# A decoder layer with routed experts: gates found at the routed steps, last rows turned by TensorE, returned rows loaded in pairs and combined by VectorE alone

## The reference

```python
x = _layernorm(x + _L0_xattn_ref(x, ctx_1024, L0_xattn_learnable_matrix), axis=-1)
x = _layernorm(x + _L0_ffn_ref(x, ...), axis=-1)

def _L0_ffn_ref(x, shared_w1, shared_w2, experts_w1, experts_w2, gate_w):
    shared = jnp.einsum('td,dh->th', x_flat, shared_w1.T)
    shared = jnp.einsum('th,hd->td', jax.nn.silu(shared), shared_w2.T)
    gate_logits = x_flat @ gate_w.T
    top_k_gates, top_k_idx = jax.lax.top_k(gate_logits, TOP_K)
    top_k_gates = jax.nn.softmax(top_k_gates, axis=1)
    gates = gates.at[jnp.arange(T)[:, None], top_k_idx].set(top_k_gates)
    h = jnp.einsum('td,ehd->teh', x_flat, experts_w1)
    expert_out = jnp.einsum('teh,edh->ted', jax.nn.silu(h), experts_w2)
    selected = jnp.einsum('ted,te->td', expert_out, gates)
    return (shared + selected).reshape(B, S, D)
```

## Time and profile before

| | us |
|---|---|
| median of 3 runs | 852.23 |
| lowest, highest | 851.64, 852.59 |
| the profiled execution | 854.55 |
| its span in the trace | 852.4 |
| TensorE matmul busy | 793.0 (93%) |
| VectorE busy | 549.4 (64%) |
| ScalarE busy | 525.1 (62%) |
| GpSimd busy | 313.4 (37%) |

### The profile page before, as it was taken

The page is one execution under the profiler, slowest core; times in us unless marked ns, Lnnn a source line. Parts: engine busy times, 40 slices in busy tenths (PEclk is TensorE's granted clock), DMA queues, the critical chain, the costliest instruction groups (busy, mean ns, idle before and its releaser), DMA issues. The chain is left out here.

```text
span 852.4 us, 19205 instructions
## 1 busy us (share of the span) xinstructions
PE 793.0 (93%) x7234; PEld 480.1 (56%) x7235; DVE 549.4 (64%) x1019; ACT 525.1 (62%) x788; POOL 313.4 (37%) x233
## 2 busy tenths in 40 slices
PE   5899999999999999999999796899999999999992
PEld 2367333333333333333332585788888888877871
DVE  4575789999999999999970495873333333212365
ACT  4441687777887787777889486454444444423475
POOL 5040594555433335555550112042333333310153
PEclk9999899999999999999999998999999999999997
DMA  9683244234344443334132697743432222212342
GB/s 298 123 217 141 111 150 137 94 102 137 132 149 150 149 149 116 100 116 172 59 113 112 250 368 179 303 82 63 76 80 74 74 74 74 70 52 66 97 148 98
DMA packets 72647, 111.95 MB, mean 131 GB/s; under 512 B 41725, under 2 KB 56254, under 8 KB 68222
## 3 DMA queue, kind: packets, MB, share of 16 engines
q1 hardware_dynamic: 67422, 93.88, 36.3%
q0 software_dynamic: 4816, 16.65, 5.7%
q10 hardware_dynamic: 336, 0.40, 0.4%
HBM read 66.60 MB, written 32.37 MB: 116 GB/s over the span
## 5 line engine op out<-in xcount | busy, mean ns | idle before, releaser
L169 DVE TENSOR_REDUCE partial<-ring 128x1 f32<-128x512 f32 (+3 forms) x509 | 308.8, 668 | 30.8 <-PE ring L151 21.6
L692 ACT ACTIVATE probs<-scores 128x1024 f32<-128x1024 f32 (+1 forms) x320 | 271.2, 905 | 63.4 <-PE scores L739 32.6
L755 PE MATMUL acc<-probs,values 128*32 128x512 f32 (+3 forms) x1280 | 170.1, 541 | 0.9 <-ACT acc_sb L697 0.7
L1666 DVE TENSOR_TENSOR work<-hid,work 128x512 f16<-128x512 f32 (+1 forms) x112 | 76.1, 682 | 136.3 <-ACT work L1269 112.9
L1264 ACT ACTIVATE hid<-turned 128x512 f32<-128x512 f32 (+1 forms) x112 | 65.3, 583 | 148.9 <-PE turned L1423 117.4
L1448 PE MATMUL ops<-weights,work 128*128 (+1 forms) x1320 | 149.5, 273 | 5.6 <-DVE work L1666 3.0
L151 PE MATMUL ring<-kstack,qstack 48*128 48x512 f16 (+1 forms) x580 | 144.8, 352 | 2.2
L1423 PE MATMUL turned<-mats,weights 128*128 128x256 f16 (+1 forms) x1344 | 144.6, 262 | 2.3 <-DMA mats<-attn 1.2
L1448 PEld LDWEIGHTS ops<-weights,work 128*128 128x128 f16 x1320 | 127.9, 98 | 22.9 <-issue 3.8
L667 POOL TENSOR_TENSOR a_w_in<-a_w_in,w_scale 128x2304 f32<-128x2304 f32 x16 | 64.4, 4027 | 207.2 <-DMA a_w_in<-w_all 207.2
L1423 PEld LDWEIGHTS turned<-mats,weights 128*128 (+1 forms) x1344 | 122.6, 98 | 21.3 <-issue 4.0
(11 more groups left out here) (201 smaller groups left out, 714.4 us busy)
## 6 DMA issues: line engine op xcount, KB each, us to landing
a_w_in<-w_all SPq DMA_DIRECT2D x16, 1152.0 KB, 7.9
w_split_d<-a_w_out SPq DMA_DIRECT2D x16, 1152.0 KB, 5.6
weights<-w_split_d SPq DMA_DIRECT2D x6, 2048.0 KB, 20.2
weights<-w_split_d POOLq DMA_DIRECT2D x3, 2048.0 KB, 11.1
qstack<-q_split SPq DMA_DIRECT2D x72, 64.0 KB, 2.6
kstack<-k_split SPq DMA_DIRECT2D x72, 64.0 KB, 2.7
weights<-by_token SPq DMA_DIRECT2D x16, 256.0 KB, 5.5
attn<-xT SPq DMA_DIRECT2D x4, 512.0 KB, 7.6
```

Source lines behind the costliest of these rows:

```text
L169: return nc.vector.tensor_reduce(out=found[:, places[0]:places[-1] + 1:step], in_=bank[:, 0:WIDTH[n]].rearrange("p (k w) -> p k w", k=len( ...
L692: nc.scalar.activation(probs[:, s % 2, at:at + w], scores[half][:, first:first + w], ACT.Exp, scale=QK_SCALE).then_inc(exp_done, 1)
L755: mm = nc.tensor.matmul(acc[VW * j:VW * (j + 1), QB - w:QB], values[:, h, k0 + j], probs[:, s % 2, at:at + w], start=first, stop=last)
L1666: nc.vector.tensor_tensor(hid[:, parity, 1, chunks, 0:w], hid32[:, b % 2].rearrange("p (j n) -> p j n", n=TW)[:, :, 0:w], hid[:, parity, 0 ...
```

## The change

1. The last item of the second layer norm no longer feeds the gates by DMA. TensorE turns its f32 rows (`turn_last`), VectorE splits them into `lastT`, and `multiply_gates` reads them there. ScalarE's first halves of these rows come behind step 1's hidden halves, the second halves move from VectorE to GpSimd, and SyncE has two transposing DMAs fewer; its store of the last quarter of `rows_d` waits for those second halves.
2. The exponential is taken at step `H0` on ScalarE, the gates are found at step `H0 + 1` on VectorE.
3. The one-hot columns are made by 16 tensor_scalar operations with a scalar per partition instead of one or two over all tiles. A few other small operations of VectorE change their form (`nmean`, `f_veps`, `f_nmean`).
4. A token's two results lie side by side in `by_token`, and one load brings both for a chunk: 8 loads of 512 KB. Four of them stand ahead of the turn for step 27.
5. VectorE multiplies by the gates and adds in one operation for each tile and choice. `scale` on ScalarE and the adding on GpSimd are gone.
6. Chunks are combined in steps 24, 25 and 26 (2, 3 and 3), and the final scaling of chunks 0 to 4 stands in steps 25 and 26.

```diff
+        lastT = region(QB, DC * QB).bitcast(f16).rearrange("p (a c n) -> p a c n", a=2, c=DC)
-        part16 = sb("part16", [P, 2, 2, NT], f16)
+        part32 = sb("part32", [P, 2, 2, NT], f32)
-        returned = weights[:, 0, 0:NC * 2 * TB * D * 2].bitcast(f32).rearrange("p (c r t d) -> p c r t d", c=NC, r=2, t=TB)
+        returned = weights[:, 0, 0:NC * 2 * TB * D * 2].bitcast(f32).rearrange("p (c t r d) -> p c t r d", c=NC, r=2, t=TB)
+        last_ps = ops[1][:].rearrange("p t d -> p (t d)").rearrange("p (c n) -> p c n", c=DC)
-        SCALED_IN = {F0: (0, 1), F0 + 1: (2, 3, 4, 5), F0 + 2: (6, 7)}
-        COMBINED_IN = {F0 + 1: (0, 1, 2, 3), F0 + 2: (4, 5, 6, 7)}
+        COMBINED_IN = {F0: (0, 1), F0 + 1: (2, 3, 4), F0 + 2: (5, 6, 7)}
+        FINAL_IN = {F0 + 1: (0, 1), F0 + 2: (2, 3, 4)}
...
@@ SyncE
-            for n in range(NC):
-                if n < LAST_HALVES:
-                    sp.wait_ge(x16_lo, n + 1)
-                else:
-                    sp.wait_ge(x16_lo_last, n - LAST_HALVES + 1)
+            for n in range(LAST_HALVES):
+                sp.wait_ge(x16_lo, n + 1)
...
             for g in range(NQ):
+                sp.wait_ge(x16_lo, (g + 1) * TPQ // TB)
...
+            def take_back(c):
+                sp.dma_start(returned[:, c], by_token[c * TW * 2:(c + 1) * TW * 2, :].rearrange("(t p r) d -> p t r d", p=P, r=2)
+                             ).then_inc(returned_in[c], 16)
+
-            for n in range(R0, NALL):
+            for n in range(R0, NALL - 1):
                 step(n, n % 2)
-
             for i in range(2):
                 sp.wait_ge(rows_out[i], 16 * sum(groups(n) for n in range(R0, F0) if n % 2 == i))
-            for c in range(NC):
-                for r in range(2):
-                    sp.dma_start(returned[:, c, r],
-                                 by_token[r * S + c * TW:r * S + (c + 1) * TW, :].rearrange("(t p) d -> p t d", p=P)
-                                 ).then_inc(returned_in[c], 16)
+            for c in range(NC // 2):
+                take_back(c)
+            step(NALL - 1, (NALL - 1) % 2)
+            for c in range(NC // 2, NC):
+                take_back(c)
@@ GpSimd
-            pool.wait_ge(allT_in[NC - 1], 16)
+            pool.wait_ge(allT_in[LAST_HALVES - 1], 16)
             for e in range(LOADED_FIRST, NE - 2):
                 load_expert(nc.gpsimd, e, late_in)
+            for n in range(LAST_HALVES, NC):
+                pool.wait_ge(x16_hi, n + 1)
+                second_halves_of_rows(nc.gpsimd, n).then_inc(x16_lo, 1)
...
-            for c in range(NC):
-                pool.wait_ge(scaled, 2 * TB * (c + 1))
-                nc.gpsimd.tensor_tensor(returned[:, c, 0], returned[:, c, 0], returned[:, c, 1], ALU.add).then_inc(pair_added, 1)
-                if c >= 2:
-                    find_scale(c - 2, (c - 2) * TB, (c - 1) * TB)
-            find_scale(NC - 2, (NC - 2) * TB, (NC - 1) * TB)
+            for c in range(NC - 1):
+                find_scale(c, c * TB, (c + 1) * TB)
@@ ScalarE
-                if n >= NQ:
+                if NQ <= n < NM - 1:
                     first_halves(n - NQ)
...
-                if isinstance(n, int) and n in SCALED_IN:
-                    for c in SCALED_IN[n]:
-                        scale(c)
-                if isinstance(n, int) and n == F0 + 2:
-                    for c in range(FINAL_AHEAD):
+                if isinstance(n, int) and n == 0:
+                    first_halves(NQ - 1)
+                if isinstance(n, int) and n == H0:
+                    act.wait_ge(gap_found, 1)
+                    nc.scalar.activation(gap_exp[:], gap[:], ACT.Exp).then_inc(gap_exp_done, 1)
+                if isinstance(n, int) and n in FINAL_IN:
+                    for c in FINAL_IN[n]:
                         final(c)
@@ TensorE
+            def turn_last():
+
+                pe.wait_ge(added, NM)
+                pe.wait_ge(ln_done, NM)
+                for c in range(DC):
+                    for t in range(TPQ):
+                        mm = nc.tensor.transpose(last_ps[:, c, t * P:(t + 1) * P], res[:, NT - TPQ + t, c * P:(c + 1) * P], ident32[:])
+                mm.then_inc(last_turned, 1)
+
...
             widen(0, 0)
+            turn_last()
             in_turn(pe, step, 0, NALL)
@@ VectorE
-                nc.vector.tensor_tensor(nmean[:, n % 2], nought[:].broadcast_to([P, TPQ]), mean_var[:, n % 2, :, 0],
-                                        ALU.subtract).then_inc(nmean_done, 1)
+                nc.vector.tensor_scalar(nmean[:, n % 2], mean_var[:, n % 2, :, 0], -1.0, None, ALU.mult).then_inc(nmean_done, 1)
...
+                for t in range(NT):
+                    one_hot = nc.vector.tensor_scalar(in_column[:, r, t], columns16[:, 0], part32[:, 0, r, t:t + 1], None, ALU.is_equal)
+                then(one_hot)
...
             def combine(c):
-                dve.wait_ge(pair_added, c + 1)
+
+                dve.wait_ge(returned_in[c], 16)
+                dve.wait_ge(gates_step, 3)
...
-                nc.vector.tensor_tensor(res[:, tiles], res[:, tiles], returned[:, c, 0], ALU.add).then_inc(combined, 1)
+                for r in range(2):
+                    for t in range(TB):
+                        tile = c * TB + t
+                        if r == 1:
+                            dve.wait_ge(combined, c * 2 * TB + t + 1)
+                        nc.vector.scalar_tensor_tensor(out=res[:, tile], in0=returned[:, c, t, r], scalar=gates[:, r, tile:tile + 1],
+                                                       in1=res[:, tile], op0=ALU.mult, op1=ALU.add).then_inc(combined, 1)
...
+                if isinstance(n, int) and n == H0 + 1:
+                    find_gates()
+
+            dve.wait_ge(last_turned, 1)
+            nc.vector.tensor_copy(lastT[:, 0], last_ps).then_inc(last_hi, 1)
+            dve.wait_ge(last_hi, 1)
+            nc.vector.tensor_tensor(lastT[:, 1], last_ps, lastT[:, 0], ALU.subtract).then_inc(last_lo, 1)
...
-            find_gates()
             in_turn(dve, step, 0, NALL)
```

More of the change, by code:

```diff
@@ L1275, in final @@
                                          scale=f_rstd[:, t:t + 1]).then_inc(act_final, 1)
-            def scale(c):
-                act.wait_ge(returned_in[c], 32)
-                for r in range(2):
-                    for t in range(TB):
-                        tile = c * TB + t
-                        nc.scalar.activation(returned[:, c, r, t], returned[:, c, r, t], ACT.Copy,
-                                             scale=gates[:, r, tile:tile + 1]).then_inc(scaled, 1)
             def step(n, parity):
@@ L1708, in find_moments @@
                 dve.wait_ge(f_aggr_done, last_tile)
[L1709 to L1712 removed]
+                nc.vector.tensor_scalar(f_veps[:, tiles], f_mean_var[:, tiles, 1], EPS, None, ALU.add).then_inc(f_var_done, 1)
+                nc.vector.tensor_scalar(f_nmean[:, tiles], f_mean_var[:, tiles, 0], -1.0, None, ALU.mult).then_inc(f_nmean_done, 1)
             def step(n, parity):
```

67 lines of the change are left out of this document (24 added, 43 removed).

## The result

The changed kernel took 844.16 us (median of 4 runs, 843.48 to 845.32), the kernel before, run beside it, 852.41: a ratio of 0.990, 95% interval 0.989 to 0.992. Forecast were 846.3. Run once more later, beside other kernels, it took 846.38 (6 runs, 843.66 to 848.99; ratio 0.993, 0.991 to 0.995). The ten runs together have a median of 844.9. The difference between the two medians is itself a finding of this study (experiments 9 and 10).

What follows compares the result with a forecast made beforehand. The prediction took TensorE alone to bound 566 to 818 us, with small routing work in the head and VectorE in the tail. Head -3.0 and tail -2.9 took 5.9 off the median 852.23: 846.3, range 843 to 848.5.

Steps and rivals of the forecast that it cites:

- both halves: The head (routing up to step 4) gains 3.0 us and the tail (combining returned rows) 2.9; chance 0.55.
- (1): Head: ScalarE's last two first halves, 1.15 us, move later; step 0's SiLU starts at 521.35 instead of 522.5.
- (3): Head: ScalarE no longer stands at the exponential, so placing starts at 536.4 instead of 540.01, -3.6 us.
- (4): Head: finding the gates leaves VectorE, 0.6 us, making -4.2; two later table loads cost nothing.
- (2): Head: TensorE's eight transposes fit its idling; choosing starts at 529.25 instead of 531.01, -1.75 us.
- (5): Head: GpSimd's last two second halves run beside placing and stall VectorE, +1.2 us.
- (6): Head: each one-hot, as 16 small operations, takes 1.5 us, -0.8 each; range -0.8 to +1.2 each.
- (7): Head: nmean and f_veps as one-input tensor_scalar count 0, with -2.2 us kept for the range.
- (8): Tail: the last send lands at 801.2, the first load pair takes 6.4 us, the first chunk starts at 807.6.
- (9): Tail: ScalarE's scaling and GpSimd's adding vanish; VectorE pays +6.8 us in all, 3.0 a chunk (2.7 to 3.3).
- (10): Tail: with chunks spread over steps 24 to 26, take 26 starts at 837.3 instead of 840.14; tail -2.9 us.
- Rival E: Slower: VectorE, alone with the returned rows, becomes the tail's bound; 854.3 us with no head gain; chance 0.07.

Runs made afterwards that it cites:

- experiment 9: Changed kernel with one-hots as before and last halves moved earlier: 843.1 us; beside it the changed kernel (846.38) and before (851.63) were run and profiled again.
- experiment 10: Experiment 9's combined version plus eight idle TensorE matmuls behind narrowing 2: 841.89 us, ratio 0.988.
- experiment 5: Changed kernel with the exponential between step 0's and step 1's SiLU and the gates found before spreading, as before: 847.07 us, ratio 0.994.
- experiment 6: Changed kernel with the last rows turned by DMA and their second halves on VectorE, as before: 844.51 us, ratio 0.990.
- experiment 4: Changed kernel with all eight loads of returned rows behind the turn for step 27: 849.41 us, ratio 0.996.
- experiment 3: Changed kernel with VectorE combining in steps 25 and 26 only, final scaling of chunks 0 to 3 in step 26: 849.9 us, ratio 0.998.
- experiment 7: Changed kernel with one-hot columns by one or two broadcast operations, as before: 844.19 us, ratio 0.991.
- experiment 2: Changed kernel with the tail of before (ScalarE scales, GpSimd adds, separate loads), so the head's change alone: 849.54 us, ratio 0.997.
- experiment 8: Changed kernel with the last rows' first halves between step 0's banks and GpSimd's second halves beside choosing: 843.69 us, ratio 0.990.

## Why the prediction was right, and where it was not

The forecast, 846.3 with both halves paying, was the case that came true; 844.16 lies in its own range of 843 to 848.5, and the second median, 846.38, on the forecast itself. That the sum is this close is in part luck: in the first profile the head gave 1.9 for 3.0 and the tail 6.5 for 2.9, two misses that go against each other. In the second pair of profiles it was 0.7 and 4.0, with 1.7 of slower clock in step 4.

(1), (3), (4) held: ScalarE without the exponential, hidden halves in time, placing 3.1 earlier for 3.6, 0.6 less on VectorE without the gates, two table loads without effect. Experiment 5 prices (3) and (4) at 2.4 when taken back.

(2) was -1.3 for -1.75: the eight transposes took 1.94 us where I had 1.5, VectorE's cast stands behind them, and between the logits' copy and choosing there are 0.75 us where I had half a one. Experiment 6 has 2.3 for the whole part before its stall, of which 1.1 is a slower clock in that execution.

(5) was 1.7 where I took 1.2, the single stall "and a little". It was two stalls, 0.83 at the cast and 0.89 at the hidden halves, together less than the 2.3 that I had for two. The range held it.

**(6) failed.** I took 0.09 us apart from two operations of 128x32 in 0.27. It was 0.16 (2.69 for 16): the 128x128 copy's 0.13, which I had set aside, was the nearer row, and it was still too low. The reason given for the smaller row, a quarter of the bytes, was wrong too: 128 f16 numbers are 256 bytes, twice those of 32 f32 and half those of 128 f32. The Trainium skill ("VectorE: DVE Perf Modes", the TRN2 errata) advised against such small tiles, with an estimate of 0.19 each and 3.0 for 16 by its constants; the trace agrees that the small tiles cost more, 2.69 against 2.28, and lies below the estimate. My sum had -1.6 for it, and it was +0.7. Of the 3.3 us by which the token numbers missed the forecast, 2.3 are this.

(7) held. `nmean` as tensor_scalar still waits for GpSimd, VectorE and GpSimd of the changed kernel:

```profile
509.13 2.27 POOL L1064 TENSOR_TENSOR weights<-res,weights 128x512 f16<-128x512 f32 x2 [2.87 <-ACT weights L1245]
509.17 1.15 DVE L1496 TENSOR_SCALAR nmean<-mean_var 128x4 f32<-128x4 f32 x1
```

1.15 us for four numbers, as 1.07 in the earlier trace rows. The Trainium skill ("SBUF — State Buffer", "Who interferes with whom") lists tensor_scalar and cast among what can take both ports; the cast of 1.03 in (5) is the same case, and the trace agrees for both. The delays I added for the gather (+1) and the clock (+0.6) were not in the first profile: from token numbers to step 4 it took 8.7 us, and 9.3 before (9.7 in its second profile). Delays of this kind come and go: 9.7 us and a widening of 7.08 in the changed kernel's second profile, 10.2 in experiment 4. The last loads of experts 7 and 6 moved 426 to 433 GB/s from 550 to 555 us in both profiles of the changed kernel and in experiment 4, but 429 and 424 also in experiments 3 and 7, where from token numbers to step 4 it took 8.6; whether they are what delays the gather was not settled.

**(8) was the term that made the difference.** From step 4's start I had the first chunk at 241.2 us; it was at 237.7, 3.4 earlier. 1.0 of it is the send, which had landed within 1.5 us of its issue where I took 2.2, near the middle of a bound 5 us wide; 2.4 are the load, 512 KB within 4.0 us, where I kept 6.4 from a pair of loads with fourteen behind it. I had named larger pieces as a reason for less and left it in the range alone. But the 6.4 was also a slow one of its kind. The same first pair, scaled by ScalarE, in the second profile of before (asked for at 801.77) and in experiment 2 (asked for at 800.38):

```profile
807.40 3.30 ACT L1282 ACTIVATE weights<-weights,gates 128x256 f32<-128x256 f32 x8 [5.75 <-DMA weights<-by_token]
```

```profile
805.17 3.51 ACT L1284 ACTIVATE weights<-weights,gates 128x256 f32<-128x256 f32 x8 [4.90 <-DMA weights<-by_token]
```

That is 5.6 and 4.8 us, and in experiment 4 one load of 512 KB with seven behind it took 5.1. So the size of the pieces is not shown to be what made the load quick; a single row had priced the term. What I missed altogether was that with the loads in their old place VectorE itself would have stood before the first chunk (experiment 4).

(9) held: 2.85 a chunk in a range of 2.7 to 3.3, with 0.40 between operations where I had 0.34, and `f_veps` at 0.17 without a stall. That GpSimd's adding was the cause and not the form of the instruction is shown by experiment 2, where `f_veps` is a tensor_scalar and GpSimd still adds:

```profile
817.94 1.09 DVE L1719 TENSOR_SCALAR f_veps<-f_mean_var 128x2 f32<-128x2 f32 x1
```

Before, as tensor_tensor, it took up to 1.08. The waiting has gone to GpSimd, whose power operation for the scale takes 0.9 instead of 0.7 us beside VectorE's two-input operations, and nobody waits for it there.

(10) held to 0.2 us: from first chunk to take 26 forecast 29.7, measured 29.5. All but 0.2 of the tail's surplus is that of (8).

Rival E needed a first chunk after 809 and 3.3 us each. Experiment 4, with the first chunk at 806.57, is the nearest to it, and its median is still 2.9 below that of before; in experiment 3 VectorE is the bound of the tail and the tail's gain is nil, but nothing is lost.

## What to carry to other kernels

Where an engine idles ahead of the piece that ends the program, moving work into the idle time pays more than relieving another engine, and it pays only as far as the transfer that feeds it is asked for early: find what stands ahead of that request on its queue, and what that waits for. Price a small operation repeated n times from the spacing of the nearest row of the same size, not from a smaller one, and a transfer from more than one profile: the same first loads took 4.8 to 6.4 us here. When two-input work is moved to GpSimd, look for what VectorE does in those microseconds. After a head is shortened, look at TensorE's idle ahead of the next dense stretch: in two of four profiles with a longer idle the stretch behind it ran at a slower clock. And profile a kernel twice before a microsecond between two last parts is explained.

## What the runs showed of the hardware that was not expected

TensorE's granted clock fell behind short idles in some executions and not in others, and the length of the idle does not tell which. Ahead of the second sort and widening 3, an idle of 3.47 us in the changed kernel's first profile was followed by 48 matmuls in 6.51 us, and one of 3.46 in its second by the same in 5.40; idles of 1.74 and 1.78 (experiments 6 and 8) were followed by 7.07. Ahead of step 4, idles of 3.20 and 1.98 were followed by 7.08, idles of 2.20 and 2.14 by 5.41.

Something further ahead goes with it. The first 24 matmuls of step 1's widening took 3.3 to 3.4 us or 4.5 to 4.7 us in the ten profiles in which TensorE turns the last rows. In the five with the short time widening 3 was slow (6.49 to 8.11 us); in the five with the long time it took 5.40. What ties the two was not found. With eight idle matmuls in the gap the granted clock was 1.00 where it was 0.69 without, in one execution each.

The falls explain part of the spread between runs of one kernel, 843.5 to 849.0 us; that they are all of it was not shown.
